# Last batch of a cross-attention kernel: transposes in two banks, inverse roots in three column groups

## The chip, the cores and the metric

The kernel runs on one core of a Trainium2 chip. The metric is the device time of one execution in microseconds (us), lower is better. The core's engines run their own instruction queues side by side and wait for each other on semaphores: TensorE (PE: matrix products and transposes, results in PSUM banks), VectorE (DVE), ScalarE (ACT), GpSimd (POOL) and SyncE (SP, which issues most DMAs).

## What is computed

```python
# B=16 batches, S=112 rows, C=320 channels, H=20 heads of 16; 371 text tokens and 4 ip tokens, E=512
q = heads(x @ W_q); k_t = heads(text @ W_k); v_t = heads(text @ W_v)
probs_t  = softmax(q @ k_t.T * 16 ** -0.5)            # per head: 112 x 371
text_out = probs_t @ v_t
qsem     = l2norm(probs_t @ text)                     # per head: 112 x 512, only its norm and its
sem      = qsem @ l2norm(ip).T                        # products with the 4 ip tokens are needed
probs_ip = softmax(q @ (ip @ W_k_ip).T * 16 ** -0.5 + 0.5 * sem) * mask[:, None]
out      = (text_out + probs_ip @ heads(ip @ W_v_ip)) @ W_out + b_out + x
```

## The kernel before

A batch is worked in NB = 18 steps. Each step treats one block of 128 rows: the 112 rows of one head and, for steps 0 to 13 (NBX = 14), 16 rows of one of the two last heads; steps 14 to 17 have the 112 rows alone. In step t the engines issue, each in its own order:

- PE: `scores(t+3)` into one of two banks; `transposes(t+1)`, three fp32 transposes of the probabilities into the one bank `ps_pT`; `products(t)`, twelve products: the Gram products of the transposed probabilities (`ps_gram`) and the value products (`ps_val`).
- ACT: `probs_hi(t+1)` copies `ps_pT` to fp16 (`pT_hi`), `exps(t+3)` makes the probabilities and the 4 ip scores (`meta`), `halve(t+1)` a halved fp16 copy; after the last step of a column group (`GROUPS` = 0:6, 6:12, 12:14, 14:18) `half_out` copies the group's values from `ps_val` to `raw`.
- DVE: `minimum(t+3)`, `probs_lo(t+1)` (what fp16 left of `ps_pT`, `pT_lo`), `quadratic(t)` (the squared norm, from `ps_gram` and `dual`, into `meta`).
- POOL: `duals(t+1)`, probabilities less their halved copy.

`transposes(t+1)` waits for `s_pT_lo` of step t, since both use `ps_pT`. `products(t)` waits for `pT_lo` of step t and for `quadratic(t-2)`; `quadratic(t)` waits for `products(t)` and `duals(t)`.

Around these steps stands the softmax of the batch ahead (batch 14 while batch 15 runs), with its values in 20 columns, one a head. POOL adds the value halves (`sum_values`, line 577); DVE makes four short `norms` (lines 1227 to 1232); POOL takes inverse roots with a pow (`inverse_roots`, line 580); DVE goes through nine more steps of `soft` with an exponential on ACT between them. The first 14 columns (`EARLY`) are done at the end of the own batch: values in step 14, norms in steps 15 and 16, pows in 16 and 17; the other 6 follow in the next batch. Four `finish` steps on PE (steps 11, 13, 15, 17) turn the result of the batch ahead into the output, in the banks `ps_prep[1]` and `ps_prep[0]` by turns. In all batches but the last, PE also prepares the next batch in `ps_prep` (the pieces of `make`). Batch 15, the last, has nothing to prepare; its body holds instead `turn_vip` (step 2), a split on POOL (step 3) and `project_vip` (step 5), which multiply the last batch's ip values by W_out ahead of time.

The `tail` ends batch 15: POOL sums the last 6 columns and makes the last two pows; DVE makes the norms and `text_out`; PE transposes `text_out`, multiplies by W_out, transposes `fprob` and adds its product; DVE makes `out_sb` and ACT stores it. `keep_busy` issues products on PE that nobody reads, in the numbers of `BUSY`, between these. Each queue's order is written out by hand; a semaphore's count is the number of operations of its kind since the start.

Of the kernel before, what the change touches and what calls it, by code (L numbers as in the profile page):

```python
# [132 lines left out]
def build(nc, x, x_t, ctx_t, ip, ip_t, mask, w_q, w_k, w_v, w_k_ip, w_v_ip, w_out, b_out, out):  # L133
# [6 lines left out]
    with stack:  # L140
# [352 lines left out]
        def _(pool):  # L493
# [114 lines left out]
            def body(b, prepare, turning, finishing):  # L608
                for t in range(NB):
# [37 lines left out]
        def _(pe):  # L647
# [139 lines left out]
            def finish(f, k, made):  # L787

                bank = ps_prep[(k + 1) % 2]
                pe.wait_ge(s_prep_lo, made)  # L790
                if k < NF - 1:
                    reached(pe, s_fin_ev, NF * f.n + k)
                if k == 0:
                    pe.wait_ge(s_soft, SOFT * (f.n + 1))
# [90 lines left out]
            def turn_vip():  # L885
# [574 lines left out]
```

## Time and profile before

| | us |
|---|---|
| median of 3 runs | 735.98 (735.73 to 736.08) |
| the profiled execution, its own time | 736.63 |
| its span in the profile | 734.8 |
| PE busy | 714.3 (97%) |
| DVE busy | 633.8 (86%) |
| ACT busy | 559.3 (76%) |
| POOL busy | 418.3 (57%) |

The profile is of one execution. Start times count from the span's start. A line of the timeline has an instruction's start, its length, the engine, the line of the code, what it writes and reads and, in brackets, how long the engine stood idle before it and for whom. Busy shares of PE include the products of `keep_busy`. Batch 15 begins near 687 and its last products end near 723.5.

### The profile page before, as it was taken

The numbers are of one execution on the slowest core, as the hardware profiler recorded it, in microseconds if no ns is written. First come the engines' busy times: TensorE is split into PE (matmuls) and PEld (weight loads), VectorE is DVE, ScalarE is ACT, GpSimd is POOL, SyncE is SP. The second block draws the span as 40 slices with busy tenths as digits, with TensorE's granted clock in tenths as the row PEclk, the third lists the DMA queues.
The fourth block names the chain that finished last, engine by engine and source line by source line (L and its number), as shares of the span: only waits on it lengthen the run. The fifth ranks groups of instructions, "written<-read, shape, count | busy, mean of one in ns | idle before, by whom it ended". The sixth has DMA issues, their size and how long they took to land.

```text
span 734.8 us, 22507 instructions
## 1 busy us (share of the span) xinstructions
PE 714.3 (97%) x7213; PEld 560.7 (76%) x7213; DVE 633.8 (86%) x1878; ACT 559.3 (76%) x1595; POOL 418.3 (57%) x516
## 2 busy tenths in 40 slices
PE   7798999999999999999999999999999999999897
PEld 5467778777787877888787878878788787877765
DVE  4478898989989898998989899898989989898985
ACT  5368787787878788787877878787787878777772
POOL 7234656556565655656465565646556464654754
PEclk9999999999999999999999999999999999999999
DMA  9656354353625435272543537254352724326001
GB/s 275 126 152 124 79 90 115 56 107 77 136 76 95 106 53 116 70 141 75 88 113 53 113 74 141 70 90 116 51 114 74 141 71 82 73 41 124 12 2 22
DMA packets 137059, 68.57 MB, mean 93 GB/s; under 512 B 77056, under 2 KB 136880, under 8 KB 136944
## 3 DMA queue, kind: packets, MB, share of 16 engines
q1 hardware_dynamic: 132368, 64.39, 41.3%
q10 hardware_dynamic: 4576, 2.74, 1.4%
q8 instruction: 61, 1.00, 0.6%
q14 instruction: 54, 0.44, 0.2%
HBM read 40.38 MB, written 15.24 MB: 76 GB/s over the span
## 4 chain that ended last, share of the span: by engine, by line
PE 88%; DMA 3%; SPq 3%; DVE 2%; ACT 2%; issue 1%; POOL 1%; ACTq 0%; DVEq 0%; POOLq 0%
PE ps_gram L761 18%; PE ps_prep L654 18%; PE ps_pT L744 12%; PE ps_gram L762 12%; PE ps_score L736 6%; PE ps_prep L715 5%; PE ps_val L770 4%; PE ps_val L771 2%; PE ps_prep L712 1%; PE ps_prep L800 1%; DMA ctx_sb<-in_ctx_t 1%; PE ps_prep L685 1%; PE ps_prep L687 1%; DMA w_raw<-in_L_xattn_W_k_ip 1%; PE ps_prep L811 1%
## 5 line engine op out<-in xcount | busy, mean ns | idle before, releaser
L573 POOL TENSOR_TENSOR dual<-prob 128x371 f32<-128x371 f32 (+1 forms) x288 | 251.7, 874 | 291.2 <-ACT prob L1013 291.2
L761 PE MATMUL ps_gram<-gram_hi,pT_hi 125*128 125x371 f16 (+1 forms) x864 | 272.3, 320 | 0.1
L762 PE MATMUL ps_gram<-gram_lo,pT_hi 125*128 125x371 f16 (+2 forms) x864 | 230.1, 267 | 0.0
L1007 ACT ACTIVATE pT_hi<-ps_pT 125x384 f16<-125x384 f32 (+1 forms) x288 | 139.1, 483 | 112.1 <-PE ps_pT L744 103.8
L1206 DVE TENSOR_TENSOR pT_lo<-ps_pT,pT_hi 125x384 f16<-125x384 f32 (+1 forms) x288 | 155.2, 539 | 31.6 <-ACT pT_hi L1007 27.1
L997 ACT ACTIVATE prob<-ps_score,low 128x371 f32<-128x371 f32 (+1 forms) x288 | 165.7, 575 | 20.6 <-DVE low L1201 15.5
L1201 DVE TENSOR_REDUCE low<-ps_score 128x1 f32<-128x371 f32 (+1 forms) x288 | 154.9, 538 | 16.4 <-PE ps_score L736 11.6
L1219 DVE CUSTOM_DVE_ANT_0 quad_junk<-ps_gram,dual 128x371 f32<-128x371 f32 (+1 forms) x288 | 153.2, 532 | 4.9 <-PE ps_gram L762 2.0
L770 PE MATMUL ps_val<-val,pT_hi 125*128 125x84 f16 (+3 forms) x864 | 152.3, 196 | 0.0
L1013 ACT ACTIVATE prob<-prob 128x371 f16<-128x371 f32 (+1 forms) x288 | 151.5, 526 | 0.0
L744 PE MATMUL ps_pT<-ident,prob 128*125 128x128 f32 (+1 forms) x864 | 142.0, 273 | 7.8 <-DVE pT_lo L1206 4.0
L744 PEld LDWEIGHTS ps_pT<-ident,prob 128*125 128x125 f32 (+1 forms) x864 | 129.9, 187 | 20.7 <-issue 7.9
L771 PE MATMUL ps_val<-val,pT_lo 125*128 125x42 f16 (+3 forms) x864 | 141.2, 181 | 0.0
L770 PEld LDWEIGHTS ps_val<-val,pT_hi 125*128 125x128 f16 (+1 forms) x864 | 80.2, 96 | 45.4
L761 PEld LDWEIGHTS ps_gram<-gram_hi,pT_hi 125*128 125x128 f16 (+1 forms) x864 | 84.3, 98 | 10.3 <-DVE gram_lo L1144 0.3
L762 PEld LDWEIGHTS ps_gram<-gram_lo,pT_hi 125*128 125x128 f16 (+1 forms) x864 | 83.9, 97 | 9.5 <-issue 2.6
L771 PEld LDWEIGHTS ps_val<-val,pT_lo 125*128 125x128 f16 (+1 forms) x864 | 79.1, 97 | 15.5
L580 POOL TENSOR_TENSOR nrm<-nrm,minus_half 112x7 f32<-112x7 f32 (+1 forms) x48 | 69.1, 1441 | 2.0 <-DVE nrm L1232 0.3
L654 PE MATMUL ps_prep<-w_hi,text_lo 128*128 128x320 f16 x184 | 54.9, 298 | 0.0
L654 PE MATMUL ps_prep<-w_lo,text_hi 128*128 128x320 f16 x184 | 54.8, 298 | 0.0
L654 PE MATMUL ps_prep<-w_hi,text_hi 128*128 128x320 f16 x184 | 54.7, 297 | 0.0
L1001 ACT ACTIVATE meta<-ps_score 128x4 f32<-128x4 f32 (+1 forms) x288 | 51.5, 179 | 0.0
(252 smaller groups left out, 1466.2 us busy)
## 6 DMA issues: line engine op xcount, KB each, us to landing
ctx_sb<-in_ctx_t SPq DMA_DIRECT2D x15, 750.0 KB, 4.8
w_raw<-k_bounce SPq DMA_DIRECT2D x32, 216.0 KB, 3.9
k_st<-k_bounce SPq DMA_DIRECT2D x28, 216.0 KB, 4.1
k_bounce<-k_hi SPq DMA_DIRECT2D x15, 288.0 KB, 4.3
k_bounce<-k_lo SPq DMA_DIRECT2D x15, 288.0 KB, 4.3
q_st<-q_bounce SPq DMA_DIRECT2D x60, 63.0 KB, 2.4
xt_sb<-in_x_t SPq DMA_DIRECT2D x16, 168.0 KB, 4.9
k_st<-k_hi SPq DMA_DIRECT2D x32, 84.0 KB, 3.1
```

What stands on the lines that cost most here:

```text
L573: nc.gpsimd.tensor_tensor(dual[0:r, t % 2, :], prob[0:r, g % 4, 0:TX], prob_16[0:r, t % 2, :], ALU.subtract).then_inc(s_dual, 1)
L654: last = nc.tensor.matmul(dst, parts_l(a, c), parts_r(b_, c), start=(n == 0), stop=(n == total - 1))
L744: last = nc.tensor.transpose(ps_pT[0:TC, i * r:(i + 1) * r], prob[0:r, g % 4, i * TC:(i + 1) * TC], ident[0:r, 0:r])
L761: nc.tensor.matmul(ps_gram[t % 2][:, 0:TX], hi, gh[0:TROWS[i], i, :], start=(i == 0), stop=False, skip_group_check=True)
L762: last = nc.tensor.matmul(ps_gram[t % 2][:, i * TC:TX], hi, gl[0:TROWS[i], i, i * TC:TX], start=False, stop=(i == NT - 1), skip_group_chec ...
L770: nc.tensor.matmul(out_, pT_hi[0:r, t % 2, i, :], v[0:r, i, heads, :], start=(i == 0), stop=False, skip_group_check=True)
L771: last = nc.tensor.matmul(out_[:, :, 0:VW], pT_lo[0:r, t % 2, i, :], v[0:r, i, heads, 0:VW], start=False, stop=(i == NT - 1), skip_group_c ...
L997: nc.scalar.activation(prob[0:r, g % 4, 0:TX], ps_score[t % 2][0:r, 0:TX], ACT.Exp, bias=low[0:r, g % 4:g % 4 + 1], scale=-1.0).then_inc(s ...
L1013: nc.scalar.activation(prob_16[0:r, t % 2, :], prob[0:r, g % 4, 0:TX], ACT.Copy, scale=0.5).then_inc(s_prob_16, 1)
L1201: nc.vector.tensor_reduce(low[0:r, g % 4:g % 4 + 1], ps_score[t % 2][0:r, 0:TX], AX.X, ALU.min).then_inc(s_low, 1)
L1206: nc.vector.tensor_tensor(pT_lo[:, t % 2, :, 0:r], ps_pT[0:TC, 0:NT * r].rearrange("p (c s) -> p c s", s=r), pT_hi[:, t % 2, :, 0:r], ALU. ...
L1219: nc.vector.tensor_tensor_reduce(out=quad_junk[0:r, :], in0=ps_gram[t % 2][0:r, 0:TX], in1=dual[0:r, t % 2, :], scale=1.0, scalar=0.0, op0 ...
```

## The change

Only batch 15 and the tail are touched (`f.n == B - 2` is batch 14, finished there).

- `turned`: in batch 15 the transposes of odd steps go to `ps_prep[1]`, those of even steps to `ps_pT`. `transposes` waits for `s_pT_lo` two steps back instead of one (step 1 for the last preparation).
- `finish_bank`: the four finish steps of batch 14, `turn_vip` and its reader use `ps_prep[0]` alone; each finish step waits for DVE's read of the one before.
- `LAST_GROUPS`: the group 14:18 is split into 14:16 and 16:18, with a `half_out` each. Their places in `ps_val` stay.
- `last_early` (POOL) and `last_norms` (DVE) replace the early part in batch 15: values 0:12 in step 12 and 12:16 in step 16; norms of 0:12 in step 13, of 12:16 in steps 16 and 17; pows of four columns in steps 14, 15, 16 and 17. The tail keeps four columns, 16:20.
- In the tail DVE makes `attn_lo` behind the fused steps of `soft` instead of ahead; `BUSY` goes from (14, 5, 9, 2) to (11, 5, 4, 2).

```diff
+LAST_GROUPS = (*GROUPS[:3], (NBX, NBX + 2), (NBX + 2, NB))
-BUSY = (14, 5, 9, 2)
+BUSY = (11, 5, 4, 2)
...
+LAST_EARLY, LAST_MIDDLE = 12, 16
+LAST_VALS_STEPS = {12: (0, LAST_EARLY), 16: (LAST_EARLY, LAST_MIDDLE)}
+LAST_POWS = {14: (0, 4), 15: (4, 8), 16: (8, 12), 17: (LAST_EARLY, LAST_MIDDLE)}
+LAST_NORMS = {(13, 0): (0,), (13, 1): (1,), (13, 2): (2, 3), (16, 2): (0, 1), (17, 0): (2, 3)}
...
+        def turned(b, t):
+            return ps_prep[1] if b.n == B - 1 and t % 2 else ps_pT
+        def finish_bank(f, k):
+            return ps_prep[(k + 1) % 2 if f.n < B - 2 else 0]
...
+            def last_early(b, step):
+                if step in LAST_POWS:
+                    pool.wait_ge(s_early, EARLY_STEPS * (b.n + (1 if LAST_POWS[step][1] <= LAST_EARLY else 2)))
+                    inverse_roots(*LAST_POWS[step])
+                if step in LAST_VALS_STEPS:
+                    h0, h1 = LAST_VALS_STEPS[step]
+                    pool.wait_ge(s_half, len(GROUPS) * b.n + (2 if h1 == LAST_EARLY else 4))
+                    pool.wait_ge(s_text_out, b.n)
+                    pool.wait_ge(s_soft, SOFT * (b.n - 1) + SOFT_ARGS)
+                    sum_values(h0, h1).then_inc(s_early, 1)
...
             def tail(b):
-                end(b.last(), VALS_STEP)
-                inverse_roots(*EARLY_POWS[NB - 1])
-                end(b.last(), POW_STEP)
+                f = b.last()
+                pool.wait_ge(s_half, len(GROUPS) * f.n + len(LAST_GROUPS))
+                pool.wait_ge(s_moved, MOVED * B)
+                sum_values(LAST_MIDDLE, H).then_inc(s_vals, 1)
+                pool.wait_ge(s_soft, SOFT * f.n + SOFT_NORMS)
+                inverse_roots(LAST_MIDDLE, H)
...
                 pe.wait_ge(s_prob, g + 1)
-                reached(pe, s_pT_lo, g)
+                if b.n < B - 1 or t == 0:
+                    reached(pe, s_pT_lo, g)
+                elif t == 1:
+                    pe.wait_ge(s_prep_lo, NM * B)
+                else:
+                    pe.wait_ge(s_pT_lo, g - 1)
...
+            def last_norms(b, k, middle):
+                dve.wait_ge(s_early, EARLY_STEPS * (b.n + middle) + k + 1)
+                h0, h1 = (LAST_EARLY, LAST_MIDDLE) if middle else (0, LAST_EARLY)
+                if k == 0:
+                    dve.wait_ge(s_quad, NB * b.n + h1)
+                    dve.wait_ge(s_text_out, b.n)
+                norms(b, k, h0, h1).then_inc(s_early, 1)
...
+                for k in range(SOFT_NORMS, SOFT_ARGS):
+                    soft(f, k)
                 dve.wait_ge(s_last_hi, 1)
                 rest = (CC - 1) * S
                 nc.vector.tensor_tensor(attn_lo[:, :, :].rearrange("p c s -> p (c s)"), ps_pT[:, 0:rest],
                                         attn_hi[:, 0:CC - 1, :].rearrange("p c s -> p (c s)"), ALU.subtract).then_inc(s_last_lo, 1)
-                for k in range(SOFT_NORMS, SOFT_ARGS):
-                    soft(f, k)
```

POOL's queue from the residual of step 11 (`x_bias`) to the end, before (`vals` is `sum_values`, a pow is `nrm<-nrm,minus_half`):

```order
L544 TENSOR_TENSOR x_bias<-x_sb,bias_sb 112x320 [waits s_fin_ev,s_x1]
L573 TENSOR_TENSOR dual<-prob,prob_16 128x371 [waits s_quad,s_prob_16]
L573 TENSOR_TENSOR dual<-prob,prob_16 112x371 [waits s_quad,s_prob_16] x2
L577 TENSOR_TENSOR vals<-raw 112x294 [waits s_soft,s_text_out,s_half]
L573 TENSOR_TENSOR dual<-prob,prob_16 112x371 [waits s_quad,s_prob_16] x2
L580 TENSOR_TENSOR nrm<-nrm,minus_half 112x7 [waits s_early]
L577 TENSOR_TENSOR vals<-raw 112x126 [waits s_moved,s_half]
L580 TENSOR_TENSOR nrm<-nrm,minus_half 112x7
L580 TENSOR_TENSOR nrm<-nrm,minus_half 112x6 [waits s_soft]
```

The same stretch of POOL's queue after:

```order
L590 TENSOR_TENSOR dual<-prob,prob_16 128x371 [waits s_quad,s_prob_16]
L594 TENSOR_TENSOR vals<-raw 112x252 [waits s_soft,s_text_out,s_half]
L590 TENSOR_TENSOR dual<-prob,prob_16 112x371 [waits s_quad,s_prob_16] x2
L597 TENSOR_TENSOR nrm<-nrm,minus_half 112x4 [waits s_early]
L590 TENSOR_TENSOR dual<-prob,prob_16 112x371 [waits s_quad,s_prob_16]
L597 TENSOR_TENSOR nrm<-nrm,minus_half 112x4 [waits s_early]
L590 TENSOR_TENSOR dual<-prob,prob_16 112x371 [waits s_quad,s_prob_16]
L597 TENSOR_TENSOR nrm<-nrm,minus_half 112x4 [waits s_early]
L594 TENSOR_TENSOR vals<-raw 112x84 [waits s_soft,s_text_out,s_half]
L597 TENSOR_TENSOR nrm<-nrm,minus_half 112x4 [waits s_early]
L594 TENSOR_TENSOR vals<-raw 112x84 [waits s_moved,s_half]
L597 TENSOR_TENSOR nrm<-nrm,minus_half 112x4 [waits s_soft]
```

The first sum of values moved from behind the third dual of this stretch to behind the first; two of the five pows now stand between duals, and the second sum of values stands behind the third pow.

DVE's queue from the `pT_lo` of step 17 to the first norm of the tail, before:

```order
L1206 TENSOR_TENSOR pT_lo<-ps_pT,pT_hi 125x3x112 [waits s_pT_hi]
L1219 ISA quad_junk,meta<-ps_gram,dual 112x371 [waits s_quad,s_dual,s_gram]
L1219 ISA meta 112x1
L1232 TENSOR_SCALAR nrm<-nrm 112x14 [waits s_early]
L1303 SCALAR_TENSOR_TENSOR out_sb<-ps_prep,x_bias 112x320 [waits s_store,s_fin]
L1219 ISA quad_junk,meta<-ps_gram,dual 112x371 [waits s_quad,s_dual,s_gram]
L1219 ISA meta 112x1
L1227 RECIPROCAL rsum<-vals 112x6 [waits s_moved,s_text_out,s_quad,s_vals]
```

The same stretch of DVE's queue after:

```order
L1245 TENSOR_TENSOR pT_lo<-ps_prep,pT_hi 125x3x112 [waits s_pT_hi]
L1258 ISA quad_junk,meta<-ps_gram,dual 112x371 [waits s_quad,s_dual,s_gram]
L1258 ISA meta 112x1
L1266 RECIPROCAL rsum<-vals 112x4 [waits s_text_out,s_quad,s_early]
L1268 TENSOR_TENSOR nrm<-meta,rsum 112x4 [waits s_early]
L1270 TENSOR_TENSOR nrm<-nrm,rsum 112x4 [waits s_early]
L1271 TENSOR_SCALAR nrm<-nrm 112x4 [waits s_early]
L1351 SCALAR_TENSOR_TENSOR out_sb<-ps_prep,x_bias 112x320 [waits s_store,s_fin]
L1258 ISA quad_junk,meta<-ps_gram,dual 112x371 [waits s_quad,s_dual,s_gram]
L1258 ISA meta 112x1
```

Four norms of the middle columns now stand between the quadratic of step 16 and that of step 17, the first of them waiting for POOL's second sum of values (`s_early`).

DVE's queue from the minimum of step 16 to that of step 17, after; before, it read the same without the four operations on 12 columns (lines 1266 to 1271):

```order
L1240 TENSOR_REDUCE low<-ps_score 112x1 [waits s_prob,s_score]
L1266 RECIPROCAL rsum<-vals 112x12 [waits s_text_out,s_quad,s_early]
L1245 TENSOR_TENSOR pT_lo<-ps_pT,pT_hi 125x3x112 [waits s_pT_hi]
L1342 TENSOR_TENSOR attn<-ps_prep,text_out 112x320 [waits s_text_out,s_fin]
L1268 TENSOR_TENSOR nrm<-meta,rsum 112x12 [waits s_early]
L1258 ISA quad_junk,meta<-ps_gram,dual 128x371 [waits s_quad,s_dual,s_gram]
L1258 ISA meta 128x1
L1270 TENSOR_TENSOR nrm<-nrm,rsum 112x12 [waits s_early]
L1271 TENSOR_SCALAR nrm<-nrm 112x12 [waits s_early]
L1240 TENSOR_REDUCE low<-ps_score 112x1 [waits s_prob,s_score]
```

The first norm, which waits for POOL's first sum of values, moved to the front of step 13's `pT_lo`.

## Rows read from the trace of the kernel before

**Rows 1.** Timeline of PE, steps 6 to 9 of batch 15: start, length, what.

```profile
700.62 0.32 PE L736 MATMUL ps_score<-w_raw,q_st 128*128 128x375 f16 x1
700.78 0.49 PE L744 MATMUL ps_pT<-ident,prob 128*125 128x128 f32 x3
...
704.77 0.56 PE L744 MATMUL ps_pT<-ident,prob 128*125 128x128 f32 x3
...
706.16 0.32 PE L736 MATMUL ps_score<-w_raw,q_st 128*128 128x375 f16 x1
706.60 0.56 PE L744 MATMUL ps_pT<-ident,prob 128*125 128x128 f32 x3
```

**Rows 2.** Chain that ended last, in order of time: start, length, engine, tile, line.

```profile
698.16 1.54 PE ps_prep L902 x9
...
713.26 0.49 ACT pT_hi L1007
...
714.48 0.55 PE ps_pT L744 x3
```

**Rows 3.** Timeline of POOL, DVE and ACT, steps 0 to 2 of batch 15.

```profile
690.13 0.84 POOL L573 TENSOR_TENSOR dual<-prob 128x371 f32<-128x371 f32 x1
...
691.10 0.55 DVE L1219 CUSTOM_DVE_ANT_0 quad_junk<-ps_gram,dual 128x371 f32<-128x371 f32 x1
...
692.56 0.56 ACT L997 ACTIVATE prob<-ps_score,low 128x371 f32<-128x371 f32 x1
```

**Rows 4.** Timeline of POOL and DVE, steps 11 to 14 of batch 15.

```profile
713.44 0.84 POOL L573 TENSOR_TENSOR dual<-prob 128x371 f32<-128x371 f32 x1 [1.59 <-ACT prob L1013]
714.24 0.87 POOL L544 TENSOR_TENSOR x_bias<-x_sb,bias_sb 112x320 f32<-112x320 f32 x1
715.06 0.84 POOL L573 TENSOR_TENSOR dual<-prob 128x371 f32<-128x371 f32 x1
...
715.55 0.51 DVE L1206 TENSOR_TENSOR pT_lo<-ps_pT,pT_hi 125x336 f16<-125x336 f32 x1
...
716.99 0.54 DVE L1201 TENSOR_REDUCE low<-ps_score 112x1 f32<-112x371 f32 x1
...
718.68 0.90 POOL L573 TENSOR_TENSOR dual<-prob 112x371 f32<-112x371 f32 x1 [0.42 <-ACT prob L1013]
```

**Rows 5.** POOL's groups by shape: count | busy us, mean ns of one.

```profile
L580 POOL TENSOR_TENSOR nrm<-nrm,minus_half 112x6 f32<-112x6 f32 x16 | 21.5, 1345 | 0.1
...
L577 POOL TENSOR_TENSOR vals<-raw 112x294 f32<-112x294 f32 x16 | 11.7, 728 | 0.0
...
L577 POOL TENSOR_TENSOR vals<-raw 112x126 f32<-112x126 f32 x16 | 6.6, 413 | 0.5 <-DMA meta<-meta_bounce 0.5
...
L557 POOL TENSOR_TENSOR ip_norm<-ip_norm,minus_half 64x1 f32<-64x1 f32 x1 | 0.6, 557 | 8.2 <-DVE ip_norm L1353 8.2
```

**Rows 6.** Timeline of the tail, all engines.

```profile
723.43 2.39 PE L883 MATMUL ps_score<-w_raw,q_st 128*128 128x375 f16 x14
...
724.53 2.80 POOL L580 TENSOR_TENSOR nrm<-nrm,minus_half 112x7 f32<-112x7 f32 x2
724.61 0.19 DVE L1227 RECIPROCAL rsum<-vals 112x6 f32<-112x6 f32 x1 [0.48 <-POOL vals L577]
...
725.89 0.51 PE L915 MATMUL ps_pT<-ident,text_out 112*128 112x112 f32 x3
...
726.97 0.39 DVE L1416 TENSOR_TENSOR attn_lo<-ps_pT,attn_hi 128x224 f16<-128x224 f32 x1 [1.13 <-ACT attn_hi L1129]
...
727.41 0.18 DVE L1261 TENSOR_TENSOR nrm<-nrm,rsum 112x20 f32<-112x20 f32 x1
```

**Rows 7.** Timeline of PE in the setup: idle time in brackets.

```profile
27.12 0.45 PE L654 MATMUL ps_gram<-w_hi,text_hi 128*128 128x320 f16 x1 [2.66 <-DVE k_lo L1141]
```

**Rows 8.** Window: busy PE, PEld, DVE, ACT, POOL; then granted clock, DMA share, GB/s.

```profile
27.00:28.00 1.00, 0.88 (x4) 0.53 (x5) 0.80 (x4) 0.00 (x0) 0.08 (x1) 0.50 0.63 152
```

**Rows 9.** Timeline of DVE, step 4 of batch 15: an operation on 20 columns.

```profile
697.85 1.09 DVE L1261 TENSOR_TENSOR nrm<-nrm,rsum 112x20 f32<-112x20 f32 x1
```

More of the change, by code:

```diff
@@ L101, in rows, with groups, group @@
     return P if t < NBX else S
-def group(t):
-    return next(n for n, (t0, t1) in enumerate(GROUPS) if t0 <= t < t1)
+def groups(b):
+    return GROUPS if b.n < B - 1 else LAST_GROUPS
+def group(b, t):
+    return next(n for n, (t0, t1) in enumerate(groups(b)) if t0 <= t < t1)
 def column(t):
-    return (t - GROUPS[group(t)][0]) * BW
+    return (t - next(t0 for t0, t1 in GROUPS if t0 <= t < t1)) * BW
 def place(a, k):
@@ L787, in finish @@
             def finish(f, k, made):
-                bank = ps_prep[(k + 1) % 2]
+                bank = finish_bank(f, k)
                 pe.wait_ge(s_prep_lo, made)
-                if k < NF - 1:
+                if k < NF - 1 or f.n == B - 2:
                     reached(pe, s_fin_ev, NF * f.n + k)
+                if k == 0 and f.n == B - 2:
+                    pe.wait_ge(s_vip_out_ev, 1)
                 if k == 0:
@@ L890, in turn_vip @@
                 for c in range(CC):
-                    last = nc.tensor.transpose(ps_prep[1][0:channels(c), c * VR:(c + 1) * VR],
+                    last = nc.tensor.transpose(ps_prep[0][0:channels(c), c * VR:(c + 1) * VR],
                                                vip_diag[:, B - 1, c * P:c * P + channels(c)], ident[0:VR, 0:VR])
@@ L1255, in soft @@
                         reached(dve, s_text_out, f.n)
-                    last = norms(f, k, EARLY, H)
+                    last = norms(f, k, EARLY if f.n < B - 1 else LAST_MIDDLE, H)
                 elif k == 4:
-                    dve.wait_ge(s_rn, POWS * (f.n + 1))
+                    dve.wait_ge(s_rn, POWS * (f.n + 1) if f.n < B - 1 else POWS * f.n + len(LAST_POWS) + 1)
                     reached(dve, s_fin_exp, f.n)
@@ L1287, in finish @@
             def finish(f, k):
-                bank = ps_prep[(k + 1) % 2]
+                bank = finish_bank(f, k)
                 dve.wait_ge(s_fin, NF * f.n + k + 1)
@@ L1374, in body, with normally @@
                 later = 0 if prepare else SOFT_LATER
+                def normally(t, place):
+                    if not prepare:
+                        for k in LAST_NORMS.get((t, place), ()):
+                            last_norms(b, k, t >= LAST_MIDDLE)
                 def softly(t, place):
+                    normally(t, place)
                     if finishing and (t - later, place) in SOFT_AT:
@@ L1401, in body @@
                     for k in range(SOFT_NORMS):
-                        if t == EARLY_NORM_STEPS[k]:
+                        if prepare and t == EARLY_NORM_STEPS[k]:
                             norms_early(b, k)
```

35 lines of the change are left out of this document (18 added, 17 removed).

## The prediction

> **What bounds the kernel now.** I read the page first, then the timeline of TensorE (PE) in the last batch, the chain of waits there, the queue of GpSimd (POOL) in its last seven steps, and the tail. The change touches only batch 15 (15 of 16, counted from 0) and the tail, some 48 us of the span. T, G, H, L, E, V, D, Q and M followed by a step number stand here for that step's transposes, products, high part, low part, exponentials, halving, dual, quadratic and minimum; a range as in vals(0:12) is columns.
>
> In [rows 1] the reader is to see two clocks in one step. From T(9) at 704.77 to the next scores at 706.16 is 1.39 us, and scores to transposes takes 0.16 where nothing is awaited (700.62 to 700.78): PE could make a step in 1.55 us. It takes 1.83 (706.60 - 704.77), because with one bank T(t+1) waits for L(t): the transposes take 0.56 and a hop, and from the start of H to the next transposes it is 1.22 (713.26 to 714.48, [rows 2]), 1.8 in all. So 0.28 us of each undisturbed step is a wait that a second bank removes. It isn't the only bound. POOL and VectorE (DVE) hold the batch at two places [rows 3]: D(1) stands behind a pow until 690.13 and Q(1) follows at 691.10; and PE's products of vip_T, 698.16 [rows 2], come on the chain straight behind a row of POOL work.
>
> **The change, first part: two banks.** No instruction is added. T(t+1) needs L(t-1) in place of L(t), so it runs while G(t) waits. I carried the four queues forward with the spacings of the rows. Q(1) is still at 691.10, since D(1) waits for the pow and not for PE; M(5), behind it on DVE, gains nothing. What gains is work that H held up: E(5), which was at 692.56 [rows 3], can follow M(5) at Q(1) + 0.46 + 0.56 = 692.12, 0.44 us sooner; hence D(3), the pow behind it, D(4), the four splits and the products of vip_T, now at about 697.7. After that everything restarts from PE's G(5). DVE has three operations of 0.51 to 0.55 per step [rows 4] with little overlap, and thirteen softmax operations of the batch ahead up to step 8, so the gain stays at 0.4 until step 9 and reaches about **0.9 us at D(12)** (713.44 before, [rows 4]). Bounds: 0.4, if the late steps add nothing; 2.6, if PE never waits from 697.7 on (1.5 for the products of vip_T, six steps of 1.55, then G(11), its copy-out, V(12), and the same hops). I take 0.9, near the lower end, since the other queues and not PE decide in that recurrence.
>
> The other bank edits come to nothing I can price above 0.1: the four finish steps of batch 14 stand two PE steps apart, and their DVE reads end well ahead; T(1) now waits for the last preparation, but H(1) was waiting for the store on ScalarE anyway. The extra copy-out of group (14, 16) and PE's wait for it before the value products of step 16 are covered by T(17) and three gram products.
>
> **Second part: the early columns.** vals(0:12) moves on POOL from behind D(15) to behind D(13), and the first norm operation moves on DVE to the front of step 13's L(14). Before, D(12), the residual and D(13) start at 713.44, 714.24, 715.06 [rows 4]. vals(0:12) starts 0.80 after D(13) and takes 0.65 (252 elements, between 0.41 for 126 and 0.73 for 294, [rows 5]). So the first norm starts at D(12) + 0.80 + 0.82 + 0.80 + 0.65 + 0.04 = D(12) + 3.11, while L(14) used to start at D(12) + 2.11 (715.55). That is **a new wait on DVE**, and behind it are queued L(14), attn, Q(13), the other norms and M(17). From there to M(17): 0.25 for the first norm, 1.44 as before from L(14) to M(17) [rows 4], about 0.6 for three more norms (0.19 each, [rows 6], and hops) less idle time that they fill, 2.3 in all. M(17) is at D(12) + 5.4; it was at D(12) + 3.55. E(17), V(15) and D(15) wait for it in turn: D(15) 1.69 later, as before (716.99 to 718.68), so at D(12) + 7.05.
>
> **Third part: five pows for three.** A pow costs 557 ns for one column and 1345 for six [rows 5]: on a line between them four columns are 1.03 us. Before, 7 + 7 + 6 columns made 4.3 us, all behind D(17) (two of them 2.80 together, [rows 6]). Now it is 5 x 1.03 = 5.2 us, and two pieces stand between duals, where Q(16), Q(17) and with them PE and DVE wait for what is queued behind. POOL: D(15), pow, D(16), pow, D(17) = 3 x 0.83 + 2 x 1.03 = 4.55; D(17) ends at D(12) + 11.6. Then pow(8:12) 1.03 and vals(12:16) 0.33, and only then may DVE start the middle norms, which its queue has **ahead of the output step and Q(17)**. Two branches follow. DVE: 4 norms 0.85, output 0.42, Q(17) 0.55. POOL: the same norms, pow(12:16) 1.03, vals(16:20) 0.33; this one is later by 0.4 and ends at D(12) + 15.2. Then the last norms 0.85 and pow(16:20) 1.03: the last pow ends at D(12) + 17.05 and the first fused step follows at D(12) + 17.1. Before it was at 727.41 = D(12) + 13.97. So this part costs **3.15 us**.
>
> **Fourth part: the tail.** attn_lo goes behind six fused steps. Before it ended at 727.36, 0.05 ahead of the first of them [rows 6], so nothing is gained there; now it and the last attn_hi (0.39 and less) stand where ScalarE makes its exponential, which hides part, and cost 0.25. On PE two products, four fillers of 0.17 (2.39 / 14, [rows 6]) and two products then follow, about 1.2 us, just over what the softmax needs: 0.1 more. Sum: 3.15 + 0.35 - 0.9 = 2.6, and with hops left out above **2.7 us**. Span 734.8 + 2.7 = 737.5. The profiled execution took 736.63 and the median is 735.98; the difference is added to the median: **738.7 us**.
>
> **TensorE's clock.** PE idles longer in the tail. Its last products end near 723.5 and eleven fillers last to 725.4, but text_out, 1.28 behind the last norms' start [rows 6], lets it on only at about 729.0: 3.6 us. The setup, [rows 7, 8], shows an idle stretch of 2.66 us, and the granted clock behind it is 0.50, the 1.2 GHz level. If it falls here, transposes, fillers and products up to the softmax transpose take double until it is back; about 0.6 us reach the end, since part hides behind DVE. Not falling costs 0. I leave it out of the forecast and in the range (to 1.5).
>
> **DVE and POOL at one port.** In [rows 9] a DVE operation on 20 columns takes 1.09 us while POOL works; in the tail its like takes 0.18 (727.41) with POOL idle, and the norms at 724.61 run in 0.19 beside a pow [rows 6]. The Trainium skill, "SBUF — State Buffer", section "Who interferes with whom", says that a DVE instruction with two SBUF inputs and a GpSimd instruction that reads SBUF exclude each other for the whole instruction. By that rule the early norms of step 13 could each wait for D(14), up to 0.8 us, and the sum would be 3.5; [rows 9] agree with it. By my order of times D(14) has just ended when they come, so the sum takes nothing.
>
> **Rivals.**
> - *PE's pace carries through* (gain of 2.6 at D(12)): for it, PE's 1.55 against 1.83; against it, DVE is busy almost throughout and its restart after vip_T isn't PE's. Even so the span is 737.5 - 1.7 = 735.8; time 737.0, within 0.2%. 0.19.
> - *Faster*: the four-column pow is near its one-column price of 0.56, so that five cost 2.35 less, with the gain at its upper bound. Then 2.7 - 1.7 - 2.35 = -1.35, and attn_lo's move is free (-0.3): 734.3. It decides from a pow under about 0.65 us. Against it: 7 columns (2.80 - 1.35) take 0.1 more than 6, so the price goes with the columns. 0.14.
> - *Forecast plus the lower clock, or the port*: 739.3 to 740.2. 0.22.
> - *The banks bring nothing beyond 0.4* (ScalarE and DVE are late anyway, and the change doesn't do what it says): 739.2. It lies inside the forecast's case.
>
> **How the numbers follow.** The forecast has 0.45, its clock or port variant 0.22, no change 0.19, faster 0.14. 0.2% is 1.5 us, about what a measurement of this kernel can tell from no change. Slower by more: 0.66 (a little of the forecast's case falls short). Same: 0.20. Faster: 0.14. The range reaches from 735.3, which leaves out most of the faster case, to 740.2.
>
> **What would show it.** In the trace after: steps 3 to 11 with transposes ahead of the low part they used to follow; D(12) near 712.5; DVE idle before the first norm of 12 columns until POOL's vals, and L(14) about 0.4 later than 715.55 in spite of the gain; pows of four columns at 1.03; D(17) near 723.3; the last quadratic behind the middle norms near 726.8; PE idle ahead of the text_out transposes. I am wrong if D(12) comes before 711, if the pow is far below 1 us, or if vals(0:12) is ready before DVE asks.

## The result, and the profile after

| | before | after |
|---|---|---|
| median, us | 735.91 (733.80 to 738.28, 16 runs) | 738.53 (735.99 to 745.91, 16 runs) |
| ratio, 95% interval | | 1.0044 (1.0027 to 1.0062) |
| profiled execution, its span | 736.63, 734.8 | 745.91, 744.1 |

The changed kernel is 2.6 us slower (2.0 to 4.6 by the interval); forecast was 738.7, slower. Its profiled execution is longer than its median, mostly by its setup: the granted clock there was 0.50 from 30 to 40 us, before only from 27 to 30, and its first dual starts at 43.16 where it was at 37.91. Step 1 of batch 15 comes 5.67 us later in it. All positions below are therefore counted **from the quadratic of step 1 of batch 15**, at 691.10 before [rows 3] and at 696.77 after, in the letters of the prediction; "end" is the end of the span:

| | D(12) | D(15) | D(17) | last pow ends | end |
|---|---|---|---|---|---|
| before | 22.34 | 27.58 | 30.46 | 36.23 | 43.70 |
| after | 21.44 | 28.02 | 31.65 | 38.08 | 47.33 |

Up to D(12) the changed kernel is 0.90 ahead; it loses 2.75 from there to its last pow, and 1.78 in the tail. D(17) before, on which the table rests:

```profile
721.56 0.84 POOL L573 TENSOR_TENSOR dual<-prob 112x371 f32<-112x371 f32 x1 [0.50 <-ACT prob L1013]
```

First the gain. Timeline of PE after, steps 2 and 3: start, length, what.

```profile
697.72 0.32 PE L770 MATMUL ps_score<-w_raw,q_st 128*128 128x375 f16 x1
697.88 0.49 PE L783 MATMUL ps_pT<-ident,prob 128*125 128x128 f32 x3
...
699.36 0.32 PE L770 MATMUL ps_score<-w_raw,q_st 128*128 128x375 f16 x1
699.52 0.49 PE L783 MATMUL ps_prep<-ident,prob 128*125 128x128 f32 x3
```

The transposes stand 0.16 behind the scores in each of these steps, in banks by turns; in [rows 1] that was so at 700.78, but 0.44 (706.16 to 706.60) in another step. The losses stand on POOL. Its timeline after, from D(12), which answers to [rows 4] and [rows 6]; idle time before an operation in brackets:

```profile
718.21 0.83 POOL L590 TENSOR_TENSOR dual<-prob 128x371 f32<-128x371 f32 x1 [1.39 <-ACT prob L1052]
...
719.83 0.84 POOL L590 TENSOR_TENSOR dual<-prob 128x371 f32<-128x371 f32 x1
720.62 0.64 POOL L594 TENSOR_TENSOR vals<-raw 112x252 f32<-112x252 f32 x1
721.53 0.89 POOL L590 TENSOR_TENSOR dual<-prob 112x371 f32<-112x371 f32 x1 [0.26 <-ACT prob L1052]
724.79 0.89 POOL L590 TENSOR_TENSOR dual<-prob 112x371 f32<-112x371 f32 x1 [2.37 <-ACT prob L1052]
725.64 1.03 POOL L597 TENSOR_TENSOR nrm<-nrm,minus_half 112x4 f32<-112x4 f32 x1
...
728.42 0.84 POOL L590 TENSOR_TENSOR dual<-prob 112x371 f32<-112x371 f32 x1
729.22 1.01 POOL L597 TENSOR_TENSOR nrm<-nrm,minus_half 112x4 f32<-112x4 f32 x1
730.19 0.33 POOL L594 TENSOR_TENSOR vals<-raw 112x84 f32<-112x84 f32 x1
731.41 1.02 POOL L597 TENSOR_TENSOR nrm<-nrm,minus_half 112x4 f32<-112x4 f32 x1 [0.89 <-DVE nrm L1271]
732.40 0.33 POOL L594 TENSOR_TENSOR vals<-raw 112x84 f32<-112x84 f32 x1
733.62 1.23 POOL L597 TENSOR_TENSOR nrm<-nrm,minus_half 112x4 f32<-112x4 f32 x1 [0.89 <-DVE nrm L1271]
```

DVE's timeline after: the first norm of the early columns, then M(17), then the middle norms, Q(17) and the last norms.

```profile
721.30 0.23 DVE L1266 RECIPROCAL rsum<-vals 112x12 f32<-112x12 f32 x1 [1.12 <-POOL vals L594]
...
723.11 0.54 DVE L1240 TENSOR_REDUCE low<-ps_score 112x1 f32<-112x371 f32 x1
...
730.56 0.18 DVE L1266 RECIPROCAL rsum<-vals 112x4 f32<-112x4 f32 x1 [2.39 <-POOL vals L594]
...
731.65 0.53 DVE L1258 CUSTOM_DVE_ANT_0 quad_junk<-ps_gram,dual 112x371 f32<-112x371 f32 x1
...
732.77 0.18 DVE L1266 RECIPROCAL rsum<-vals 112x4 f32<-112x4 f32 x1 [0.58 <-POOL vals L594]
```

The loss of 2.75 splits in three: 1.34 between D(12) and D(15), where DVE waits 1.12 for POOL's values; 0.75 between D(15) and D(17), where two pows stand; and 0.66 behind D(17), where values, norms and pow of the middle and of the last columns follow each other, with POOL and DVE waiting for each other by turns (0.89, 2.39, 0.89, 0.58).

The tail after. PE's timeline, and the windows there (busy PE, PEld, DVE, ACT, POOL; then granted clock, DMA share, GB/s):

```profile
728.67 1.91 PE L922 MATMUL ps_score<-w_raw,q_st 128*128 128x375 f16 x11
734.03 0.82 PE L954 MATMUL ps_pT<-ident,text_out 112*128 112x112 f32 x3 [3.45 <-DVE text_out L1466]
734.64 1.77 PE L922 MATMUL ps_score<-w_raw,q_st 128*128 128x375 f16 x5
```

```profile
732.00:734.00 2.00, 0.00 (x0) 0.00 (x0) 1.30 (x7) 0.00 (x0) 1.11 (x3) 0.73 0.24 72
734.00:736.00 2.00, 1.97 (x8) 1.28 (x9) 0.95 (x4) 0.50 (x2) 0.85 (x1) 0.50 0.00 0
736.00:738.00 2.00, 2.00 (x9) 1.50 (x8) 1.80 (x7) 0.27 (x1) 0.00 (x0) 0.50 0.03 8
```

PE stands still for 3.45 us, and works on at a granted clock of 0.50, the 1.2 GHz level: the transposes take 0.82 instead of 0.51 [rows 6], a filler 0.35 instead of 0.17.

### The profile page after: what moved, and what is told of

Its sections match the earlier page's. It is cut to its first block, busy times and chain, and to the rows that moved or that the text cites. A ratio compares the mean times of both kernels' runs of the same rounds, so it can differ in the third digit from the quotient of the medians.

```text
span 744.1 us, 22501 instructions
## 1 busy us (share of the span) xinstructions
PE 719.8 (97%) x7205; PEld 564.4 (76%) x7205; DVE 634.1 (85%) x1882; ACT 557.6 (75%) x1596; POOL 418.7 (56%) x519
## 4 chain that ended last, share of the span: by engine, by line
PE 89%; POOL 2%; issue 2%; DVE 2%; DMA 2%; ACT 1%; ACTq 1%; SPq 0%; DVEq 0%; POOLq 0%
PE ps_prep L688 18%; PE ps_gram L800 17%; PE ps_pT L783 12%; PE ps_gram L801 11%; PE ps_score L770 6%; PE ps_prep L749 5%; PE ps_val L809 4%; PE ps_val L810 2%; PE ps_prep L746 1%; PE ps_prep L719 1%; POOL dual L590 1%; PE ps_prep L721 1%; PE ps_prep L839 1%; DMA w_raw<-in_L_xattn_W_k_ip 1%; PE ps_prep L850 1%
## 5 line engine op out<-in xcount | busy, mean ns | idle before, releaser
L1046 ACT ACTIVATE pT_hi<-ps_pT 125x384 f16<-125x384 f32 (+1 forms) x279 | 134.6, 482 | 113.6 <-PE ps_pT L783 106.3
L1245 DVE TENSOR_TENSOR pT_lo<-ps_pT,pT_hi 125x384 f16<-125x384 f32 (+1 forms) x279 | 150.2, 538 | 30.0 <-ACT pT_hi L1046 25.9
L783 PE MATMUL ps_pT<-ident,prob 128*125 128x128 f32 (+1 forms) x837 | 136.8, 272 | 3.5 <-ACT prob L1036 2.6
L783 PEld LDWEIGHTS ps_pT<-ident,prob 128*125 128x125 f32 (+1 forms) x837 | 126.7, 188 | 13.4 <-issue 4.8
L597 POOL TENSOR_TENSOR nrm<-nrm,minus_half 112x7 f32<-112x7 f32 (+2 forms) x50 | 70.0, 1400 | 3.5 <-DVE nrm L1271 1.8
```

The source lines that it names most:

```text
L783: last = nc.tensor.transpose(turned(b, t)[0:TC, i * r:(i + 1) * r], prob[0:r, g % 4, i * TC:(i + 1) * TC], ident[0:r, 0:r])
L1245: nc.vector.tensor_tensor(pT_lo[:, t % 2, :, 0:r], turned(b, t)[0:TC, 0:NT * r].rearrange("p (c s) -> p c s", s=r), pT_hi[:, t % 2, :, 0:r ...
```

## The experiments

The theory: the columns cost more than the banks give; of that, the clock is a part of its own; and the order of POOL's queue and the norms' wait are the rest. The rival: the two parts disturb each other, or five pows are simply too much work. Ratios are to the kernel before, run beside each kernel; its median beside them was 735.1 to 735.8, so medians of different rows compare only roughly. Where the time stood, from the quadratic of step 1, in all ten runs:

| kernel | D(12) | D(15) | D(17) | last pow ends | end | median, us | ratio (95%) |
|---|---|---|---|---|---|---|---|
| banks_only | 21.45 | 26.29 | 28.61 | 35.16 | 42.65 | 734.54 | 0.9989 (0.9968 to 1.0010) |
| columns_only | 22.33 | 29.52 | 33.24 | 39.67 | 47.42 | 740.07 | 1.0053 (1.0032 to 1.0074) |
| fillers30 | 21.45 | 28.04 | 31.67 | 38.10 | 45.85 | 737.90 | 1.0017 (0.9998 to 1.0036) |
| norms_late | 21.44 | 27.69 | 31.32 | 37.74 | 47.05 | 739.29 | 1.0042 (1.0019 to 1.0064) |
| pool_order | 21.45 | 28.04 | 31.66 | 36.62 | 44.37 | 736.63 | 1.0022 (1.0001 to 1.0044) |
| duals_free | 21.45 | 28.04 | 30.16 | 37.89 | 45.69 | 737.53 | 1.0031 (1.0019 to 1.0044) |
| quad_first | 21.46 | 28.05 | 31.67 | 38.11 | 45.89 | 737.30 | 1.0020 (1.0005 to 1.0035) |
| banks_norms | 21.45 | 26.30 | 28.40 | 34.85 | 42.37 | 734.69 | 0.9983 (0.9971 to 0.9995) |
| norms_psum | 21.45 | 26.31 | 28.42 | 34.46 | 42.00 | 734.34 | 0.9986 (0.9967 to 1.0005) |
| norms_psum_split | 21.45 | 26.31 | 28.41 | 34.15 | 41.81 | 734.79 | 0.9994 (0.9972 to 1.0015) |

In banks_only and duals_free the trace shows D(16) and D(17) as one group; D(17) is taken as its end less 0.84. The positions in the trace repeat to a few hundredths (D(12) in the ten kernels with two banks: 21.44 to 21.46), the ratios are known to 0.12 to 0.23%, or 0.9 to 1.7 us. So the small steps are read from the positions, each in one execution; of the ratios one is clear of 1 on the faster side (banks_norms), five on the slower (columns_only, norms_late, duals_free, quad_first, and pool_order barely), four are not.

### The banks alone

```diff
-LAST_GROUPS = (*GROUPS[:3], (NBX, NBX + 2), (NBX + 2, NB))
+LAST_GROUPS = GROUPS
...
-BUSY = (11, 5, 4, 2)
+BUSY = (14, 5, 9, 2)
...
```
with the early columns and the tail as before.

> The bank edits alone (transposes of batch 15 by turns in two banks, finish steps in one); column groups, POOL's and DVE's order, tail and fillers as before. Counted from the quadratic of step 1 in batch 15, which waits for a dual behind a pow and so doesn't move, the dual of step 12 stood 22.3 us later before and 21.4 after the whole change, and the end 43.7 before and 47.3 after. My theory (the banks gain 0.9 at the dual of step 12 and the columns cost some 3.5): dual of step 12 at 21.4, end at 42.6 to 42.9, time 0.8 to 1.1 us under before. Rival (the gain of the banks is eaten by the tail, where POOL's pows end last): end at 43.5 or more, time as before. Rival (the banks themselves cost something in steps 13 to 17): end above 44.

It ended at 42.65, 1.05 sooner than before: the banks do what they say, and their 0.9 at D(12) reaches the end. By the ratio alone, 0.9989 (0.9968 to 1.0010), it couldn't be told from no change.

### The columns alone

```diff
-            return ps_prep[1] if b.n == B - 1 and t % 2 else ps_pT
+            return ps_pT
...
-            return ps_prep[(k + 1) % 2 if f.n < B - 2 else 0]
+            return ps_prep[(k + 1) % 2]
```
and the wait for `s_pT_lo` as before.

> The column part alone (five pows of four columns, norms and value sums moved, the split group, attn_lo behind the fused steps, fillers 11, 5, 4, 2); one transpose bank and two finish banks as before. My theory: first norm of 12 columns 3.1 us behind the dual of step 12, end 3.5 us later than before, counted from the quadratic of step 1: 47.2 with TensorE's clock kept, up to 48.7 if it falls in the tail; time 739.4 to 740.9. Rival (the columns cost little and the loss after the change comes from banks and columns together): end under 45, time under 737.

End 47.42, 3.72 later than before, at full clock. Both parts together (fillers30, at full clock) cost 2.15, and 3.72 - 1.05 would be 2.67: with the columns the second bank is worth 0.5 more. Why, DVE and POOL of this kernel show (timeline):

```profile
716.70 0.85 DVE L1263 TENSOR_TENSOR nrm<-meta,rsum 112x12 f32<-112x12 f32 x1
```

```profile
716.64 0.89 POOL L590 TENSOR_TENSOR dual<-prob 112x371 f32<-112x371 f32 x1 [0.88 <-ACT prob L1047]
```

The norm product takes 0.85 and ends at 717.55, 0.02 behind D(14). With two banks D(14) stands 0.6 sooner against D(12), and the same product took 0.24. These 0.6 are the whole difference of M(17), D(12) + 5.51 here and + 4.90 after.

### Thirty fillers

```diff
-BUSY = (11, 5, 4, 2)
+BUSY = (30, 5, 4, 2)
```

> The changed kernel with 30 fillers instead of 11 behind the last products, which at 0.17 us each last until the transposes of text_out. My theory: TensorE's idle stretch of 3.45 us goes, the granted clock stays 1.00 in the tail, the products and fillers ahead of the softmax transpose take half as long, and that transpose follows the last softmax step at once: end 1.4 us sooner than after the change (45.9 instead of 47.3 from the quadratic of step 1), time 737.2 or so if most executions of the changed kernel lose the clock. Rival (the clock costs nothing at the end because DVE is as late): end as after the change, 47.3.

PE's timeline of this kernel:

```profile
720.07 4.93 PE L922 MATMUL ps_score<-w_raw,q_st 128*128 128x375 f16 x30
725.43 0.51 PE L954 MATMUL ps_pT<-ident,text_out 112*128 112x112 f32 x3 [0.42 <-DVE text_out L1466]
```

The last pow ends where it did (38.10), the transposes are back at 0.51, the end comes at 45.85 instead of 47.33. So the clock cost 1.48 in the profiled execution after. The median is only 0.6 lower, and the intervals of the two ratios overlap.

### The early norms behind step 13

```diff
-LAST_NORMS = {(13, 0): (0,), (13, 1): (1,), (13, 2): (2, 3), (16, 2): (0, 1), (17, 0): (2, 3)}
+LAST_NORMS = {(13, 2): (0, 1, 2, 3), (16, 2): (0, 1), (17, 0): (2, 3)}
```

> The changed kernel with the four norms of columns 0 to 12 all behind the quadratic of step 13 instead of the first of them ahead of step 13's low part. The value sum on POOL stays where it is. My theory (DVE's wait for POOL's sum delays the low part, the minimum of step 17 and through it the dual of step 15): the wait of 1.12 us goes, dual of step 15 at 5.9 to 6.1 us behind the dual of step 12 instead of 6.6, end 0.5 to 0.7 us sooner than after the change. Rival (the wait is slack, the end is set by POOL's own work from the dual of step 12 on): end unchanged.

The end came only 0.28 sooner, and D(15) 0.33: a miss. DVE, then POOL, of this kernel:

```profile
715.71 0.82 DVE L1268 TENSOR_TENSOR nrm<-meta,rsum 112x12 f32<-112x12 f32 x1
```

```profile
715.61 0.90 POOL L590 TENSOR_TENSOR dual<-prob 112x371 f32<-112x371 f32 x1 [0.25 <-DVE meta L1258]
```

The wait of 1.12 is gone, but the norm product now comes beside D(14) and is 0.58 longer (0.82 for 0.24). 0.33 + 0.58 is 0.9: by this sum, which no run shows by itself, that is what the wait for the values was worth.

### POOL's order

```diff
-                if step in LAST_POWS:
-                    pool.wait_ge(s_early, EARLY_STEPS * (b.n + (1 if LAST_POWS[step][1] <= LAST_EARLY else 2)))
-                    inverse_roots(*LAST_POWS[step])
...
                     sum_values(h0, h1).then_inc(s_early, 1)
+                if step in LAST_POWS and step < NB - 1:
+                    pool.wait_ge(s_early, EARLY_STEPS * (b.n + 1))
+                    inverse_roots(*LAST_POWS[step])
```
and in the tail the sum of 16:20 ahead of the pow of 12:16; 22 fillers.

> The changed kernel with two swaps in POOL's queue: the sum of values 12:16 stands ahead of the pow of columns 8:12, and the sum of values 16:20 ahead of the pow of columns 12:16; the first fillers of the tail are 22 instead of 11, so that TensorE doesn't idle. Times from the quadratic of step 1. Theory (the order of POOL's queue is the largest part of what the columns cost: each sum of 0.33 us waits behind a pow of 1.03 that nobody on DVE is waiting for): the middle norms start 1.0 sooner, the quadratic of step 17 and the last norms run beside a pow, and the last pow ends near 36.5 instead of 38.1; end near 44.3 against 45.85 for the changed kernel with its clock kept; time 1.5 below the run with thirty fillers. Rival (the five pows' own length on POOL is the bound, whatever the order): last pow 37.8 to 38.1 and end 45.6 to 45.9.

POOL's timeline of this kernel, from the values of 12:16:

```profile
721.99 0.33 POOL L594 TENSOR_TENSOR vals<-raw 112x84 f32<-112x84 f32 x1
722.28 1.02 POOL L597 TENSOR_TENSOR nrm<-nrm,minus_half 112x4 f32<-112x4 f32 x1
723.27 0.34 POOL L594 TENSOR_TENSOR vals<-raw 112x84 f32<-112x84 f32 x1
723.56 1.02 POOL L597 TENSOR_TENSOR nrm<-nrm,minus_half 112x4 f32<-112x4 f32 x1
724.93 1.22 POOL L597 TENSOR_TENSOR nrm<-nrm,minus_half 112x4 f32<-112x4 f32 x1 [0.35 <-DVE nrm L1273]
```

The last pow ends 1.48 sooner than with thirty fillers, and so does the end (44.37). No work was taken out: the two idle times of 0.89 became one of 0.35, since the norms now run beside a pow. So more than half of the 2.75 was the order of POOL's queue, not the five pows' length. The two swaps weren't run apart. The ratios don't show the step: 1.0022 here and 1.0017 with thirty fillers, each known to 0.2%.

### No pow between the duals

```diff
-LAST_POWS = {14: (0, 4), 15: (4, 8), 16: (8, 12), 17: (LAST_EARLY, LAST_MIDDLE)}
+LAST_POWS = {16: (0, 12), 17: (LAST_EARLY, LAST_MIDDLE)}
```
on top of thirty fillers.

> The changed kernel with thirty fillers and one pow of 12 columns behind the dual of step 17, in place of three pows of four, two of them between duals. Times from the quadratic of step 1. Theory (the pows that stand between duals are what delays duals 16 and 17, and a pow costs 0.4 us plus 0.158 a column): dual 17 starts at 29.9 to 30.6 instead of 31.67, the 12-column pow takes 2.3 us, so the middle norms start no sooner and the end is 45.7 to 46.2 against 45.85. Rival A (the duals wait for the late norms on DVE, not for the pows): dual 17 stays within 0.3 of 31.67 and the end comes 1.0 or more later, 46.9. Rival B (a pow's price is mostly fixed): the 12-column pow takes under 1.6 us and the end is 45.2 or sooner.

POOL's timeline of this kernel:

```profile
723.76 2.30 POOL L597 TENSOR_TENSOR nrm<-nrm,minus_half 112x12 f32<-112x12 f32 x1
```

D(17) came 1.5 sooner and the end 0.16. The pows do hold up the duals, but most of the time only moves. The price of twelve columns is the 2.30 of the line, 0.75 less than three pows of four; against that POOL now stands idle for 0.33 ahead of D(16), and the middle values start only 0.2 sooner.

### The middle norms behind the last quadratic

```diff
-(16, 2): (0, 1), (17, 0): (2, 3)}
+(17, 2): (0, 1, 2, 3)}
```
on top of thirty fillers.

> The changed kernel with thirty fillers and the four middle norms on DVE behind the quadratic of step 17 instead of ahead of it. Times from the quadratic of step 1. Theory (of the two branches from the middle values on, POOL's with the pow of 12:16 and the sum of 16:20 is the later one, so it doesn't matter what DVE does in between): the quadratic of step 17 starts 0.5 or more sooner, the middle norms and with them the fourth pow within 0.1 of where they were, end 45.8 to 46.0 against 45.85. Rival (the quadratic behind the norms is what the last norms wait for, as the prediction's words on the four norms ahead of it may be read): end 45.35 or sooner.

Q(17) on DVE in this kernel:

```profile
722.96 0.55 DVE L1258 CUSTOM_DVE_ANT_0 quad_junk<-ps_gram,dual 112x371 f32<-112x371 f32 x1 [0.82 <-POOL dual L590]
```

It came 2.25 sooner than with thirty fillers (32.65 for 34.90), the end 0.04 later. The four norms ahead of the quadratic cost nothing here.

### The banks, with the norms drawn together

```diff
-                    if prepare or t < NB - 1:
+                    if prepare or t < NB - 1 and t != EARLY_VALS_STEP:
                         end_early(b, t)
+                    if not prepare and t == EARLY_VALS_STEP - 1:
+                        end_early(b, EARLY_VALS_STEP)
...
-                        if t == EARLY_NORM_STEPS[k]:
+                        if t == (EARLY_NORM_STEPS[k] if prepare else EARLY_NORM_STEPS[0]):
```
on top of the banks alone.

> The kernel with the banks part alone and the tail of before, but the sum of values 0:14 on POOL right behind the dual of step 14, and all four early norms on DVE at their place in step 15 (before, two in step 15 and two in step 16). Times from the quadratic of step 1. Theory (in the run with the banks alone POOL idles 1.07 us ahead of the 7-column pow for the last early norm, and this idle time is on the path to the last pow): the last pow ends at 34.1 to 34.5 instead of 35.16, the end is 41.6 to 42.0 instead of 42.65, the time about 0.8 below the banks alone and 2.0 below the kernel before. Rival (the wait moves to the duals of 15 and 16, since DVE now does four short norms in one step): last pow 35.0 or later, end 42.5 to 42.9.

(Before, three of these norms stood in step 15 and one in step 16, not two and two.) The last pow ended 0.31 sooner, not 0.7 to 1.1. DVE, then POOL:

```profile
719.28 0.83 DVE L1267 TENSOR_TENSOR nrm<-meta,rsum 112x14 f32<-112x14 f32 x1
```

```profile
719.23 0.84 POOL L590 TENSOR_TENSOR dual<-prob 112x371 f32<-112x371 f32 x1 [0.19 <-DVE meta L1257]
720.60 1.51 POOL L597 TENSOR_TENSOR nrm<-nrm,minus_half 112x7 f32<-112x7 f32 x1 [0.53 <-DVE nrm L1270]
```

The same picture a third time: a norm product that starts beside a dual ends 0.04 behind it, and the pow waits 0.53. Another idle 0.41 stands ahead of the last sum of values, where POOL waits for ScalarE's copy.

### One operand in PSUM

```diff
+                if b.n < B - 1:
+                    norms(b, k, 0, EARLY).then_inc(s_early, 1)
+                    return
+                r, n = ps_score[0][0:S, 0:EARLY], nrm[:, :, 0:EARLY]
+                if k == 0:
+                    last = nc.vector.reciprocal(r, vals[:, 0:EARLY, DH])
+                elif k == 1:
+                    last = nc.vector.tensor_tensor(n[:, 0, :], meta[b.odd][0:S, 0:EARLY, 0], r, ALU.mult)
+                elif k == 2:
+                    last = nc.vector.tensor_tensor(n[:, 1, :], n[:, 0, :], r, ALU.mult)
+                else:
+                    last = norms(b, k, 0, EARLY)
...
+                nc.vector.reciprocal(rsum[:, 0:EARLY], vals[:, 0:EARLY, DH])
```
on top of the run before; the last line stands at the start of the tail.

> The kernel of the run banks_norms, but the reciprocal of the sums of the 14 early columns of the last batch is written to a free PSUM bank, so that the two norm products of these columns read one operand from SBUF and one from PSUM; the copy in SBUF that text_out needs is made later, in a gap of DVE. Times from the quadratic of step 1. Theory (a norm product with both operands in SBUF waits for a dual that runs on POOL: in banks_norms the first took 0.83 us and ended 0.04 after that dual, where its like takes 0.17 beside a pow or an idle POOL): it takes 0.25 or less, the early norms end 0.5 to 0.6 sooner, the 7-column pow follows dual 17 directly, the last pow ends at 34.3 to 34.5 instead of 34.85 and the end is 41.8 to 42.0 instead of 42.37. Rival (the length is the price of 14 columns at that place, wherever the operand lies): 0.7 or more, end 42.3 or later.

DVE, then POOL, of this kernel:

```profile
725.17 0.17 DVE L1285 TENSOR_TENSOR nrm<-meta,ps_score 112x14 f32<-112x14 f32 x1
725.38 0.17 DVE L1287 TENSOR_TENSOR nrm<-nrm,ps_score 112x14 f32<-112x14 f32 x1
725.58 0.41 DVE L1270 TENSOR_SCALAR nrm<-nrm 112x14 f32<-112x14 f32 x1
```

```profile
725.12 0.84 POOL L590 TENSOR_TENSOR dual<-prob 112x371 f32<-112x371 f32 x1 [0.19 <-DVE meta L1257]
726.07 1.51 POOL L597 TENSOR_TENSOR nrm<-nrm,minus_half 112x7 f32<-112x7 f32 x1
```

The same product, at the same place beside the same dual, takes 0.17 instead of 0.83. The last pow ended at 34.46 and the end came at 42.00, both 0.4 sooner. The last norm, a single-input operation from SBUF to SBUF, still waited: 0.41 instead of 0.17, and it ends 0.03 behind the dual. The Trainium skill, "SBUF — State Buffer", section "Who interferes with whom", has both: a VectorE instruction with two SBUF inputs, or a `tensor_scalar` in a two-port mode, excludes a GpSimd instruction that reads SBUF. The traces agree where that instruction is a dual, though no row shows in which mode the last norm ran; beside a pow, which reads SBUF as well, they don't (below).

### Ten and four columns

```diff
-                inverse_roots(*EARLY_POWS[NB - 1])
+                inverse_roots(10, EARLY)
```
and 0:10 for the pow ahead of it, on top of the run before.

> As norms_psum, but the two early pows have 10 and 4 columns instead of 7 and 7. Times from the quadratic of step 1. Theory (behind the first pow POOL waits 0.4 us or more for ScalarE's copy of the last values, so columns moved from the second pow to the first are free; a pow costs 0.4 us plus 0.158 a column): the last pow ends 0.3 to 0.45 sooner than in norms_psum, near 34.0, the end is 41.4 to 41.6, the time 733.5 to 734.0 against 735.7 to 735.9 of the kernel before. Rival (the last norms on DVE, not POOL's two pows, are what the last pow waits for): end within 0.1 of norms_psum.

POOL, then DVE, of this kernel:

```profile
718.65 1.98 POOL L597 TENSOR_TENSOR nrm<-nrm,minus_half 112x10 f32<-112x10 f32 x1
720.60 0.41 POOL L594 TENSOR_TENSOR vals<-raw 112x126 f32<-112x126 f32 x1
```

```profile
723.40 0.39 DVE L1480 TENSOR_TENSOR attn_lo<-ps_pT,attn_hi 128x224 f16<-128x224 f32 x1 [1.13 <-ACT attn_hi L1167]
723.71 0.17 DVE L1320 TENSOR_TENSOR nrm<-nrm,rsum 112x20 f32<-112x20 f32 x1
```

The last pow ended 0.31 sooner, as expected, but the end only 0.19, at 41.81 where 41.4 to 41.6 was expected: the pow is out of the way by 723.44, and the first fused step (723.71) now comes behind `attn_lo`. The median, 734.79 where 733.5 to 734.0 was expected, shows nothing of so small a step.

## Why the prediction was right

The time (738.7 for 738.53) and the sign are right, and so is the mechanism: the banks gain a little, POOL's queue with its five pows loses more. That the two times agree to 0.2 us is luck. The sum was 0.55 too large and the clock, left out, cost 1.48 in the trace; together the trace gives 3.63 for a forecast of 2.7, and the medians 2.62 with an interval of 2.0 to 4.6.

- **Banks.** 0.4 at the products of vip_T: 0.42 (6.64 for 7.06). 0.9 at D(12): 0.90. The lower end was the right choice; PE's own pace of 1.55 was not reached.
- **Early norms.** The first at D(12) + 3.11: 3.09, after an idle 1.12. M(17) at D(12) + 5.4: it was 4.90, and D(15) at 6.58 for 7.05. (5.4 and 1.69 make 7.09, not 7.05.) The term of the sum that was sized wrong is "2.3 in all" from the first norm to M(17): it was 1.81. Counted from start to start, the four norms take 0.60 of it, not 0.25 and 0.6, and L(14), attn and Q(13) take 1.21 where they took 1.44.
- **The pows.** 1.03 for four columns: 1.01 to 1.03, and 1.23 for the last. D(15) to the end of D(17) 4.55: 4.47. From there to the end of the values of 16:20 3.6: 3.47. POOL's branch is the later one there, by 0.54 where 0.4 was said (732.19 and 732.73), and quad_first shows that it decides. Last pow at D(12) + 17.05: its end came at 16.64; cost 3.15: 2.75. The 0.47 at D(15) accounts for that 0.4.
- **Tail.** 0.35: from the last pow to the end 7.47 before and 7.75 in fillers30, so 0.28.
- **Sum at full clock.** 2.7: it was 2.15 (45.85 - 43.70), of which -0.90, 2.75 and 0.28 are the three parts above.
- **Clock.** Idle of 3.6: 3.45, and the clock did fall. It was taken as 0 with 0 to 1.5 in the range, 0.6 as its size; in the profiled execution it was 1.48, the upper end. DVE didn't hide it: at 0.50 PE's own chain of fillers and products is longer than the softmax, and fprob, ready at 41.29, waited until 42.83. Leaving the clock out more than made good the 0.55 by which the sum was too large. How much every execution pays isn't settled: the medians with and without the fillers are 0.6 apart, and each ratio is known to some 0.18%, or 1.3 us, either way. The mean granted clock of the whole execution speaks for most of them losing it: it was at most 0.995 in all 28 executions of the changed kernel and of norms_late, and 0.998 in 8 of 12 with thirty fillers and in 4 of 8 of columns_only.
- **Port.** Taken as 0, since D(14) would just have ended. It had not: it ended at 722.42, and the norm product, which started at 722.20, ended at 722.44, some 0.05 longer than without a dual. In columns_only and norms_late the same wait is 0.6. The choice was right by 0.2 us of position, and the kernel's second bank is what put it there. The norm at 724.61 that the prediction sets beside a pow is the reciprocal, with one input; the two products behind it, at 724.84 and 725.04, took 0.17 each inside the same pow.
- **Rivals.** PE's pace and "banks bring only 0.4" fell with D(12); the cheap pow fell with 1.02.

A version that beats both came out, by 0.17% over the kernel before: banks_norms, 0.9983 (0.9971 to 0.9995); and by its positions norms_psum, whose end is 0.37 sooner still (42.00; before, 43.70); its ratio, 0.9986 (0.9967 to 1.0005), can't tell it from either.

## What to carry to other kernels

When work is cut into more groups so that less is left for the end, look at the queue of the engine that serves the groups: here the sum of values that the next group waits for stood behind a pow that nobody on DVE waited for, and two such changes of place were together worth 1.48 us in the trace without removing anything. Before short operations are moved, see what the engine at the other side of a shared resource does at the new place; one operand in PSUM made it harmless for the two products, though not for the `tensor_scalar` behind them. And where a change lengthens the idle time of TensorE, price the slower clock behind it on the chain that ends last, not behind the work that used to hide it.

## What the runs showed of the hardware

- A norm product of 12 or 14 columns, both inputs in SBUF, that started beside a dual on POOL took 0.82 to 0.85 us in three kernels and ended 0.02 to 0.04 behind the dual; with one input in PSUM it took 0.17 beside the same dual. In banks_only the second product took 0.76 and ended 0.03 behind D(17).
- The kernel before has this wait in every batch but the last: its fourth early norm, the `tensor_scalar` of 14 columns, took 0.82 to 0.88 us in batches 0 to 14, beside a dual that ended 0.02 to 0.04 sooner, and 0.17 in batch 15, where no dual ran. What it costs there no run shows. DVE, then POOL, of the kernel before:

```profile
81.39 0.88 DVE L1232 TENSOR_SCALAR nrm<-nrm 112x14 f32<-112x14 f32 x1
```

```profile
81.35 0.89 POOL L573 TENSOR_TENSOR dual<-prob 112x371 f32<-112x371 f32 x1 [1.84 <-ACT prob L1013]
```

- Beside a pow products of 4 and 6 columns did not wait: 0.17 in the kernel before, and 0.16 in the last norms of pool_order, the first of which stands inside its pow of 723.56 to 724.58. No run has one of 12 or 14 columns there.

```profile
724.29 0.16 DVE L1270 TENSOR_TENSOR nrm<-meta,rsum 112x4 f32<-112x4 f32 x1
724.49 0.16 DVE L1272 TENSOR_TENSOR nrm<-nrm,rsum 112x4 f32<-112x4 f32 x1
```

- A pow went by its columns: 1.02 us for 4, 1.98 for 10, 2.30 for 12; beside `text_out` the last one took 1.22 to 1.23.
- After an idle 3.45 and 3.44 us (after, norms_late) the granted clock was 0.50; after an idle 2.88 us in columns_only it stayed at 1.00 (windows of columns_only, the idle time mostly in the first). The length of the idle time doesn't settle it alone: in the setup 0.50 stands behind an idle 2.66 [rows 7, 8].

```profile
727.00:729.00 2.00, 0.00 (x0) 0.00 (x0) 1.32 (x7) 0.00 (x0) 1.11 (x3) 1.00 0.24 72
729.00:731.00 2.00, 1.77 (x12) 1.18 (x12) 0.93 (x5) 0.50 (x2) 1.05 (x1) 1.00 0.00 0
```
